# Mix stage: the triangle's weight product as two 64-row matmuls in banks of their own, and one PSUM bank for transposition and x product

## The reference, cut to what matters

```python
block = einsum('bikc,bkjc->bijc', pp, ab1) + einsum('bikc,bjkc->bijc', ab2, lp) + ab3 * ip   # 64 channels
g = sigmoid(zn @ Wend + bend)                                  # zn: layer norm of x, 128 channels
out = g * (_ln(block, lnc_g, lnc_b) @ Wsum + bsum) * zm
x = x + out
```

## Time and profile before

| | us |
|---|---|
| median of 3 runs | 1430.08 (1429.14 to 1431.77) |
| the profiled execution | 1432.56 |
| its span | 1430.8 |
| busy in the span: PE, DVE, ACT, POOL | 1349.7, 1224.4, 999.6, 998.5 |
| mix stage, 697 to 905 us | PE 191.5, DVE 191.0, POOL 159.6, ACT 134.2 |

### The profile page before, as it was taken

How to read it: one execution, slowest core, us unless ns; L and a number is a source line. 1 busy time by engine, 2 the same in 40 slices (tenths; PEclk the granted TensorE clock), 3 DMA queues, 4 the chain that set the end, 5 groups by cost and what they waited for, 6 DMA issues and landing times. The chain is left out here.

```text
span 1430.8 us, 32169 instructions
## 1 busy us (share of the span) xinstructions
PE 1349.7 (94%) x9880; PEld 1131.8 (79%) x9880; DVE 1224.4 (86%) x4099; ACT 999.6 (70%) x2327; POOL 998.5 (70%) x1559
## 2 busy tenths in 40 slices
PE   6999999999999998999699999699999999999994
PEld 3887788877788777898566666599999999999984
DVE  7999899989888974887799999667888888888897
ACT  3888888888888886555366666346766776677673
POOL 4999999999999996444388888335555555555574
PEclk9999999999999999999899999699999999999997
DMA  9999999999999998889599994311232222222213
GB/s 225 221 257 253 249 246 250 263 255 260 236 246 251 259 245 278 293 305 289 160 270 295 291 291 167 108 45 45 75 87 66 85 75 84 79 74 75 89 45 89
DMA packets 357530, 267.48 MB, mean 187 GB/s; under 512 B 60432, under 2 KB 332722, under 8 KB 357362
## 3 DMA queue, kind: packets, MB, share of 16 engines
q1 hardware_dynamic: 355800, 264.76, 69.1%
q10 hardware_dynamic: 1290, 0.46, 0.2%
q0 software_dynamic: 272, 0.21, 0.1%
HBM read 171.02 MB, written 94.37 MB: 185 GB/s over the span
## 5 line engine op out<-in xcount | busy, mean ns | idle before, releaser
L1545 ACT ACTIVATE hT<-psH_d,b 128x512 f32<-128x512 f32 x288 | 197.8, 688 | 155.1 <-PE psH_d L1585 155.0
L661 PE MATMUL psZ_a<-w_all,xT_a 128*128 128x128 f32 x1728 | 230.1, 276 | 0.1
L661 PE MATMUL psZ_a<-w_all,xT_block 128*128 128x384 f32 x576 | 214.7, 496 | 5.2 <-DVE low_ab L730 4.9
L661 PEld LDWEIGHTS psZ_a<-w_all,xT_a 128*128 128x128 f32 x1728 | 209.8, 192 | 3.0 <-ACT xT_a L569 2.3
L585 ACT ACTIVATE sig_a<-psZ_a 128x256 f32<-128x256 f32 (+1 forms) x360 | 153.5, 426 | 80.8 <-PE psZ_a L661 50.5
L597 POOL TENSOR_SCALAR shared<-shared,coefs_early 128x128 f32<-128x128 f32 x468 | 203.4, 449 | 0.0
L648 PE MATMUL psT_a<-ident,shared 128*128 128x128 f32 x1152 | 186.1, 274 | 3.4 <-issue 2.0
L648 PEld LDWEIGHTS psT_a<-ident,shared 128*128 128x128 f32 x1152 | 141.3, 142 | 54.9 <-issue 27.3
L1239 DVE TENSOR_SCALAR shared<-shared,coef 128x128 f32<-128x128 f32 x288 | 179.2, 681 | 1.6 <-POOL xh_b L1619 1.6
L1612 POOL TENSOR_TENSOR u_d<-u_d,gamma 128x512 f32<-128x512 f32 x72 | 94.3, 1310 | 118.2 <-ACT u_d L1528 116.8
L1619 POOL TENSOR_TENSOR xh_b<-shared,b 128x512 f32<-128x512 f32 x72 | 93.2, 1294 | 105.1 <-DVE ffn_sum L1680 103.9
(11 more groups left out here) (233 smaller groups left out, 3173.0 us busy)
## 6 DMA issues: line engine op xcount, KB each, us to landing
shared<-in_x_dram SPq DMA_DIRECT2D x48, 512.0 KB, 5.8
scratch_xT<-xT_block SPq DMA_DIRECT2D x36, 512.0 KB, 5.3
shared<-scratch_xT SPq DMA_DIRECT2D x36, 512.0 KB, 4.9
scratch_x<-x_c SPq DMA_DIRECT2D x36, 512.0 KB, 3.9
shared<-scratch_x SPq DMA_DIRECT2D x36, 512.0 KB, 3.6
shared<-in_x_dram SPq DMA_DIRECT2D x48, 256.0 KB, 5.2
shared<-L_conv_protein_pair_dram SPq DMA_DIRECT2D x24, 512.0 KB, 7.7
shared<-in_L_conv_l_pair_dram SPq DMA_DIRECT2D x24, 512.0 KB, 9.2
```

The costliest lines, as they stand in the source:

```text
L661: ins = nc.tensor.matmul(out, turned_x(G, i, t0, size)[:, j * P:j * P + P], rhs[i], start=True, stop=True)
L1545: nc.scalar.activation(hT[:, S % 2, f, :], psH[:, f, :], ACT.Gelu, bias=s["b1"][:, f:f + 1]).then_inc(gelued, 1)
```

## The change

`psT` is no tensor of its own any more: it is columns 256 to 383 of the bank of `psZ` with the same j % 2. The two banks so freed go to `psW`, which has four: two for each pair. W becomes two matmuls of 64 rows and 128 columns each. The first takes rows 0 to 63 of `triT` and of `ws2`, and so the upper half of the array's rows, and writes one bank; the second takes rows 64 to 127 and writes the other. The zeros of `ws2` are not multiplied any more. y reads 128 columns from each of the two banks.

Since a bank must not be written by PE while ACT reads it, two waits change. T(c) now waits for gate(c-2) too, which reads the same bank. Z(c) waits for copy(c), a wait that stood between Z(c) and W(c) before.

```diff
--- before.py
+++ after.py
@@ -962,9 +962,9 @@
         stats = sb("stats_c", [P, 2, KINDS_C, TPB, 6])
         stats_t, stats_x = stats[:, :, TRI_KIND], stats[:, :, X2_KIND]
         work = sb("work_c", [P, 6, KINDS_C, TPB])
-        psT = ctx.enter_context(nc.psum_tensor("psT_c", [P, 2, 512], F32))
         psZ = ctx.enter_context(nc.psum_tensor("psZ_c", [P, 2, 512], F32))
-        psW = ctx.enter_context(nc.psum_tensor("psW_c", [P, 2, 512], F32))
+        psT = psZ[:, :, 2 * CH:2 * CH + P]
+        psW = ctx.enter_context(nc.psum_tensor("psW_c", [P, 2, 2, 512], F32))
         chunk_sems = lambda name: [sem(f"{name}_{k}") for k in range(len(CHUNKS))]
         loaded_x = s["loaded_x"]
         stored = [chunk_sems(f"stored_x2{par}") for par in range(2)]
@@ -1050,7 +1050,7 @@
                 c = PAIRS * (2 * m + par) + j
                 act.wait_ge(turned, c + 1)
                 need(act, tri_projected, c - 1)
-                nc.scalar.copy(triT[:, j % 2, :], psT[:, j % 2, 0:P]).then_inc(copied, 1)
+                nc.scalar.copy(triT[:, j % 2, :], psT[:, j % 2, :]).then_inc(copied, 1)
 
             def slot(m, par, j):
                 c = PAIRS * (2 * m + par) + j
@@ -1104,9 +1104,10 @@
 
                 c = PAIRS * (2 * m + par) + j
                 need(pe, copied, c - 1)
+                need(pe, gated, c - 1)
                 pe.wait_ge(tri_normed_act, c + 1)
                 pe.wait_ge(tri_normed_pool, c + 1)
-                nc.tensor.transpose(psT[:, j % 2, 0:P], tri_n[:, j % 4].rearrange("p t c -> p (t c)"), s["ident"][:]
+                nc.tensor.transpose(psT[:, j % 2, :], tri_n[:, j % 4].rearrange("p t c -> p (t c)"), s["ident"][:]
                                     ).then_inc(turned, 1)
 
             def slot(m, par, j):
@@ -1120,14 +1121,17 @@
                     if 2 * j == CHUNKS[k][0]:
                         pe.wait_ge(s["loaded_xT"][par][k], 16 * (m + 1))
                     need(pe, gated, c - 1)
+                    pe.wait_ge(copied, c + 1)
                     for i in range(2):
                         ins = nc.tensor.matmul(psZ[:, j % 2, CH * i:CH * i + CH], xT_in[:, par, 2 * j + i, :], w_end,
                                                start=True, stop=True)
                     ins.then_inc(projected, 1)
-                    pe.wait_ge(copied, c + 1)
                     need(pe, y_made, c - 1)
-                    nc.tensor.matmul(psW[:, j % 2, 0:2 * CH], triT[:, j % 2, :], s["ws2"][:], start=True, stop=True
-                                     ).then_inc(tri_projected, 1)
+                    for h in range(2):
+                        half = slice(HID * h, HID * h + HID)
+                        ins = nc.tensor.matmul(psW[:, j % 2, h, 0:CH], triT[half, j % 2, :], s["ws2"][half, CH * h:CH * h + CH],
+                                               start=True, stop=True)
+                    ins.then_inc(tri_projected, 1)
 
                 if j >= ROUTE_FROM:
                     (rm, rpar), pair = last_block(m, par), j - ROUTE_FROM
@@ -1207,7 +1211,7 @@
                         dve.wait_ge(tri_projected, c + 1)
                         dve.wait_ge(gated, c + 1)
                         need(dve, x2_made, c - 1)
-                        v.tensor_tensor(y[:, j % 2], psW[:, j % 2, 0:2 * CH].rearrange("p (t c) -> p t c", t=2),
+                        v.tensor_tensor(y[:, j % 2], psW[:, j % 2, :, 0:CH],
                                         gate[:, j % 2], ALU.mult).then_inc(y_made, 1)
                     if part == 2:
                         if j > 0 and now:
```

## The result

| | before | changed |
|---|---|---|
| median, runs of both side by side | 1430.92 (1429.14 to 1432.15, 4 runs) | 1444.28 (1442.82 to 1445.51, 4 runs) |
| the profiled execution | 1432.56 | 1442.82 |
| its span | 1430.8 | 1441.1 |
| block of the mix stage, steady | 16.26 | 17.11 |
| first y to last y of the stage | 196.53 | 207.70 |

The change makes the kernel slower: the ratio of the times is 1.0094, with a 95% interval of 1.0082 to 1.0106. The forecast was 1438.0, with a range of 1431.0 to 1447.0: direction and range hold, but the cost is 13.4 us in the medians where 7.9 was worked out. The two profiled executions are 10.3 apart, and the stage alone is 11.2 longer (207.70 - 196.53), so in the profiles all of it lies in the mix stage.

The account below looks back on a forecast made before the run. DVE was taken to pace pairs 1 to 9 and PE the block's last three steps. Twelve boundaries x 0.66 = 7.9 us on the profiled 1432.56 gave 1440.5, less 2.5 for the median: 1438.0, range 1431.0 to 1447.0.

Parts of the forecast that it names:

- The switches: On PE around W: changing between full-array and half-row work leaves a hole, taken as 0.09 us, and an open weight load.
- rival 2: W on PE: row halves cost no switch, 0.51 us a boundary, +6.1 us, 1436.2; chance 0.14.
- rivals 3 and 4: W on PE: 3, half loads go one after another, 1442.6, chance 0.11; 4, halves don't run together, 1453, chance 0.08.
- Rival 5: Block's end: delay absorbed, as something (such as POOL's norm) held PE there anyway; within 2.9 us of before, 1430; chance 0.09.
- rival 6: Same three slots: PE's shorter product wins, no switch or gate wait, slot 0.78, -4 to -5 us, 1425.5; chance 0.08.
- its own case: The case as worked out: 0.66 us lost per block boundary, 1438.0, own span 1434.5 to 1440; chance 0.50.
- rival 3: W on PE: four half loads go one after another, PE sets the whole block, +12.5 us, 1442.6; chance 0.11.
- the stage's edges: Mix stage's first two pairs and last pair: same loop, priced together as one boundary more, 0.66 us.
- release by gate(9): Block's end: gate(9) ends 813.96, T(11) loads 814.07, so Z(10) starts 814.24, before 813.65.
- the loop by the gate: Block's end on PE: Z, gate, T, next Z takes 1.03 + 0.11 + 0.17 = 1.31 us, where the old slot had 1.0.
- Z(11) to Z(12), with R: Block's end: PE's slot with R takes 1.46 us, before 1.47, putting Z(12) at 817.01, before 816.33.
- The thin cover of 0.3 us: Whole block: PE's twelve slots cost 16.6 us against the new block of 16.92, so PE regains its lead.

## Why the prediction was right in direction, and too small

**What held.** DVE's pairs 1 to 8 are untouched; the three last steps are the place; T waits for the gate of its bank, and the waits alone carry the whole cost. The switches are real: holes of 0.093 on both sides, 0.09 forecast, which takes away rival 2. The Trainium skill ("TensorEngine Tiling (Array Packing)", Key Properties) says that a change of tiling mode drains the engine; the trace agrees, by these holes. The halves run together, 7 ns apart, which takes away rivals 3 and 4, although the result of the third lies near the measured time; its 12.5 us were to come from W's second half and a slot with R of 1.57, while W's halves are together and the slot is 1.52, longer than the forecast's 1.46 for another reason, Z's open load. W's result came 1.03 after Z where T had not waited (822.14 to 823.17), as forecast, and 1.09 where it had. Reading two banks cost nothing. Rival 5 fell with the three holes, rival 6 with the gate's end, 1.03 to 1.10 after Z, which is far behind PE's 0.67.

**Where luck helped.** The prediction gave its own case 1434.5 to 1440, and 1444.28 lies outside that. It lies in the range because the range was drawn up to 1447.0 for rival 3 and for halves that overlap in part, and neither happened. Of the 5.5 us that are missing, the boundaries make 2.2, the stage's edges 1.0 and the way from profile to median 3.1, less 0.9 by which the profiles differ less than the stages.

**The boundary: 0.85, forecast 0.66.** By the prediction's own steps, measured from y(8) to y(12):

| step | forecast | measured | off |
|---|---|---|---|
| y(8) to Z(10): release by gate(9) | 1.27 | 1.22 | -0.05 |
| Z(10) to Z(11): the loop by the gate | 1.31 | 1.47 | +0.16 |
| Z(11) to Z(12), with R | 1.46 | 1.52 | +0.06 |
| Z(12) to y(12) | 1.10 | 1.12 | +0.02 |

The mis-sized term is the loop's: 1.31 in the sum, 1.47 measured. It took the release of T as 0.11, from a T that waited for POOL; it was 0.07 at T(11) and 0.20 at T(12), where one more waiting instruction stood between the gate's end and the load. (In the slots where neither is added the loop is 1.27.) And it said that the moved wait, "copy(c) before Z(c), costs nothing". It never waits, but it is an instruction of PE's queue between T and Z, so that Z's first weight load lies open and every product after it comes 0.06 later, gate and W too. The run without the implied waits shows both: 1.27, even below the 1.31 that was worked out. The thin cover of 0.3 us a block that the prediction left PE was about right, 16.74 against 17.11; that is why the norm moved behind the gate gained no more than 0.29.

**The edges: 1.7, forecast 0.66.** The ten blocks from y(12) to y(132) took 8.6 more, the first block 1.6, the last eleven steps 0.95. Eleven boundaries are 9.5 of it, 1.7 remains. The sum priced the first pairs at the full clock and left out that they run at the lower level, with a loop of 1.99; y(0) to y(5) took 0.94 more. At the end it priced one pair, but the last block has a boundary's delay too: its last four steps, 0.72, 0.93, 1.40 and 0.88 before, are 1.02, 1.33, 1.46 and 1.06. The two together are 1.9, and the first block's own boundary cost 0.2 less than the others.

**From profile to median.** The sum was made against 1432.56, 2.5 over the median of three runs, and the same distance was taken off. Beside the changed kernel the median was 1430.92, 1.6 under that profile, and the profiled execution of the changed kernel is the fastest of its four, 1.5 under their median. So the profiles are 10.3 apart and the medians 13.4. A first block that varies with the clock would fit the second part, but only one of the four was profiled.

**A reason that was wrong.** The prediction explained the hole before the block's first y in the kernel before by ACT, which stands until DVE's last coefficient step and so leaves PE no lead. The order of ACT was changed and the hole stayed. It went when POOL's norm was moved a pair ahead, so it is POOL's addition and norm that held T there, a wait that the prediction had seen one pair earlier, and used for rival 5 alone. The forecast did not suffer: in the changed kernel it is gate(9), behind ACT's norm, that comes last.

## What to carry to other kernels

Before two results are put into one bank, write down which waits that creates, and close the loop: product, reader, next writer of the bank, product. If the loop is longer than the slot of the engine that writes, the bank costs the difference wherever that engine has no lead, whatever the new matmuls save; the waits can be tried alone, in the old kernel, before anything is rebuilt. And a hole is worth closing only as far as the next engine allows: here POOL's 1.07 us a pair stood right behind PE, and the time stayed.

## What the runs showed of the hardware that was not expected

- A wait that never waits can cost time on PE. With one waiting instruction more between the gate's wait and T's load, and one between T and Z, a transposition's load came 0.20 after the release and not 0.07, and a product's second pass 0.174 after its first and not 0.112. In the records the surplus waits are instructions of 0.051 us each. Dropping the implied ones gave 0.28 us a block.
- Two 64-row matmuls on the two halves of the rows start 7 ns apart, and their four passes of 128 columns take the time of two: W's record at 818.033 to R's load at 818.453 is 0.42, of which 0.107 is the open load, 0.214 two passes and 0.093 the hole. The prediction took it as open whether such loads overlap, since the section that it drew on does not say. The Trainium skill does say it elsewhere ("TensorEngine Tiling (Array Packing)", Key Properties): different tiles can load weights and multiply in parallel. The trace agrees: the two first loads start at 818.032 and 818.038, and each lasts 0.183.
- The half-row work did not pay here, between full-array work: one passage in and one out cost 0.093 each and left weight loads open (0.107 ahead of W, 0.06 more ahead of the next Z), against 0.22 us of streaming saved, and in the kernel with the halves alone the next Z came 0.14 later without R (1.13, 0.99 before).
- A wait costs DVE 0.08 to 0.09 more than the idle time in the brackets. y(10) stood 1.32 behind y(9) with a wait of 0.26, where without a wait the step was 0.98. In the kernel before, a y that does not wait starts before the record ahead of it ends (statistics 815.75 + 0.34 = 816.09, y 816.00), and the idle time is counted from that end.
